# Scaling the probability rows on ScalarE instead of VectorE in a fused attention and gated adapter kernel

## The reference, cut to what matters

```python
q = (xn @ wq.T)   # 32 heads of 128;  k, v: 8 heads of 128, each shared by 4 query heads
q, k = rope(q), rope(k)
scores = q k^T / sqrt(128) * key_scale + causal
probs  = softmax(scores)
attn   = probs @ v
s = attn @ wo.T
x = x + s * silu(mixture_of_rank_16_adapters(xn))
```

## Time and profile before

| | us |
|---|---|
| median of 3 runs | 1474.9 (1472.89 to 1476.49) |
| span of the profiled execution, from its first instruction to its last | 1473.0 |
| TensorE busy | 1372.8 (93%) |
| VectorE busy | 1196.0 (81%) |
| ScalarE busy | 809.3 (55%) |
| GpSimd busy | 423.0 (29%) |

### The profile page before, as it was taken

How to read it: one execution, slowest core, us unless ns; L and a number is a source line. 1 busy time by engine, 2 the same in 40 slices (tenths; PEclk the granted TensorE clock), 3 DMA queues, 4 the chain that set the end, 5 groups by cost and what they waited for, 6 DMA issues and landing times.

```text
span 1473.0 us, 23326 instructions
## 1 busy us (share of the span) xinstructions
PE 1372.8 (93%) x6982; PEld 1130.1 (77%) x6982; DVE 1196.0 (81%) x3022; ACT 809.3 (55%) x2064; POOL 423.0 (29%) x340
## 2 busy tenths in 40 slices
PE   6699999999998999989999999999999999999997
PEld 5577667788777887778777887778877787877785
DVE  6976768878889887888888788887787888888887
ACT  4445555555555665556555555556555565555563
POOL 4311123221434123241342213331233312423231
PEclk9799999999999999999999999999999999999999
DMA  5000021000001000000000000000000000001223
GB/s 196 22 12 1 22 72 65 22 7 0 21 21 28 0 7 21 14 28 0 14 28 21 7 0 21 21 28 0 2 26 14 28 0 14 22 13 64 79 71 136
DMA packets 23291, 43.33 MB, mean 29 GB/s; under 512 B 2464, under 2 KB 2592, under 8 KB 23264
## 3 DMA queue, kind: packets, MB, share of 16 engines
q1 hardware_dynamic: 20736, 37.90, 8.0%
q10 hardware_dynamic: 2528, 5.11, 0.9%
HBM read 34.61 MB, written 8.39 MB: 29 GB/s over the span
## 4 chain that ended last, share of the span: by engine, by line
PE 49%; issue 21%; DVE 18%; POOL 8%; ACT 3%; DMA 0%; POOLq 0%; DVEq 0%; ACTq 0%
PE o_ps L542 13%; PE bank_b L450 12%; PE bank_a L450 7%; PE s_ps L517 5%; PE pv_ps L532 4%; POOL rot L366 3%; DVE probs L1126 3%; PE t_ps L625 3%; POOL w_lo L359 3%; DVE probs L1079 2%; POOL w_hi L356 2%; PE s_ps L512 2%; DVE cosx L999 2%; DVE cosx L989 2%; DVE q_lo L1005 2%
## 5 line engine op out<-in xcount | busy, mean ns | idle before, releaser
L366 POOL TENSOR_TENSOR rot<-rot,tab 128x512 f32<-128x512 f32 x160 | 209.6, 1310 | 921.3 <-ACT rot L730 921.3
L800 ACT ACTIVATE probs<-probs,row_min 128x128 f32<-128x128 f32 (+1 forms) x512 | 227.1, 445 | 122.1 <-DVE row_min L1079 120.9
L1126 DVE TENSOR_SCALAR probs<-probs,row_inv 128x128 f32<-128x128 f32 (+1 forms) x512 | 208.5, 470 | 4.5
L450 PE MATMUL bank_b<-xT_hi,w_hi 128*128 (+1 forms) x508 | 205.3, 404 | 0.5 <-POOL w_lo L373 0.5
L542 PE MATMUL o_ps<-w_hi,attn_hi 128*128 128x512 f32 x500 | 198.9, 398 | 7.2 <-POOL w_lo L359 4.0
L450 PE MATMUL bank_b<-xT_hi,w_lo 128*128 (+1 forms) x508 | 199.8, 393 | 0.0
L450 PE MATMUL bank_b<-xT_lo,w_hi 128*128 (+1 forms) x508 | 199.2, 392 | 0.0
L542 PE MATMUL o_ps<-w_lo,attn_hi 128*128 128x512 f32 x500 | 197.3, 395 | 0.0
L542 PE MATMUL o_ps<-w_hi,attn_lo 128*128 128x512 f32 x500 | 196.8, 394 | 0.0
L761 ACT ACTIVATE attn_hi<-pv_ps 128x512 fp32r<-128x512 f32 x128 | 76.4, 597 | 172.1 <-PE pv_ps L532 171.3
L625 PE MATMUL t_ps<-tab,probs 128*128 128x128 f32 x768 | 110.9, 282 | 49.1 <-DVE probs L1126 49.0
(11 more groups left out here) (151 smaller groups left out, 3094.8 us busy)
## 6 DMA issues: line engine op xcount, KB each, us to landing
raw<-w_seq SPq DMA_DIRECT2D x78, 256.0 KB, 2.6
gate_scratch<-silu ACTq DMA_DIRECT2D x16, 256.0 KB, 2.1
out<-y_sum SPq DMA_DIRECT2D x16, 256.0 KB, 2.0
raw<-x SPq DMA_DIRECT2D x13, 256.0 KB, 2.7
raw<-gate_scratch SPq DMA_DIRECT2D x13, 256.0 KB, 2.9
x_sb<-x SPq DMA_DIRECT2D x3, 1024.0 KB, 10.6
x_sb<-x SPq DMA_DIRECT2D x4, 256.0 KB, 5.7
tab<-tables ACTq DMA_DIRECT2D x1, 768.0 KB, 5.3
```

The costliest lines, as they stand in the source:

```text
L366: nc.gpsimd.tensor_tensor(v, v, tab[:, s:s + SEQ].unsqueeze(1).to_broadcast([P, 2, SEQ]), ALU.mult).then_inc(sin_done[kind], 1)
L450: mm = nc.tensor.matmul(dst, w(a, c), x[:, c, bass.ds(x0, BLOCK)], start=(c == 0 and n == 0), stop=(c == DC - 1 and n == 2))
L800: a = nc.scalar.activation(s, s, ACT.Exp, bias=row_min[:, i:i + 1], scale=-1.0, accum_out=row_sum[:, i:i + 1])
L1126: ins = nc.vector.tensor_scalar(s, s, row_inv[:, i:i + 1], None, ALU.mult)
```

## The change

The four multiplications of `probs` by `row_inv` leave `dve_unit` and come into `act_unit`, right behind the four exponents, as activations with a Copy and the reciprocal as their scale. ScalarE waits there for `inv_done`, which VectorE's reciprocal sets; the reciprocal itself stays on VectorE, and `probs_ready` is now set by ScalarE.

```diff
@@ act_unit
                 a.then_inc(exp_done, 1)
+                act.wait_ge(inv_done, n4[j + 1])
+                for h in range(2):
+                    for qt in range(2):
+                        s = probs[:, h, P * qt:P * qt + P * (qt + 1)]
+                        i = 2 * h + qt
+                        a = nc.scalar.activation(s, s, ACT.Copy, scale=row_inv[:, i:i + 1])
+                a.then_inc(probs_ready, 1)
@@ dve_unit
                 nc.vector.reciprocal(row_inv[:, :], row_sum[:, :]).then_inc(inv_done, 1)
-                dve.wait_ge(inv_done, n4[j + 1])
-                for h in range(2):
-                    for qt in range(2):
-                        s = probs[:, h, P * qt:P * qt + P * (qt + 1)]
-                        i = 2 * h + qt
-                        ins = nc.vector.tensor_scalar(s, s, row_inv[:, i:i + 1], None, ALU.mult)
-                ins.then_inc(probs_ready, 1)
```

## The result

The changed kernel takes 1577.34 us (median of 4 runs, 1574.22 to 1577.60) against 1474.91 us before (1472.89 to 1476.49). The ratio is 1.0695, with a 95% interval of 1.0679 to 1.071: slower by 7.0%. The forecast was 1493, slower by 1.2%, with a range up to 1518. The direction was right and the size wrong by a factor of more than five.

The account below looks back on a forecast made before the run. TensorE, busy 93%, was taken as the bound, so only its waits count. Terms 36 + 3 - 11 + 3 - 11 + 2 + 2 = +24, clock -9, leaning to +18 on 1473.0, median 1.9 above: 1493 us, range 1478 to 1518.

Parts of the forecast that it names:

- stretched, not late: VectorE's scalings at the three long transposes' waits per group (2.58, 1.90, 2.32 us) take 4.85 us instead of 1.01.
- The price of the scaling: On ScalarE, four scalings in a row take 1.06 us until the next instruction starts, priced from plain Copies.
- Part 1: Item j = 1, output bank: TensorE stalls 1.12 us, or 1.30 in a group's fourth unit, +36 us in all.
- Part 2: Item j = 3, queries: 3.96 us from reciprocal to first score; changes of +3, -11 and +3 us.
- Part 3: First unit of a group: 1.2 of the 2.58 us wait comes back, -11 us over eight.
- The clock: Of 24 us lost at TensorE's lower level, 9 us come back as stretches behind long waits go.
- Rival (b): New stalls of about 1.1 us in each of 31 units also drop the clock: +40, 1533 us; chance 0.05.
- The first group: Side work shares `o_ps` there: +2 us.
- Rival (a): Stretched scalings decide: their waits and lost clock go, no query stall follows, -34, 1441 us; chance 0.21 in both sizes.
- half size: Only half the gain from removing the stretched scalings is had: 1458 us; chance 0.21 shared with the full size.
- The dear end of the scaling: Four scalings on ScalarE priced like the exponents, end to end: 1.76 us, adding 39 us.
- sign of being wrong: Forecast wrong if the scaling takes 1.5 us or more, L542 rarely waits for L1041, or calm units' clock falls below 0.97.

Follow-up runs that it names:

- e2: Changed kernel with the scaling of item j = 1 alone back on VectorE: 1530.16 us, ratio 1.0407 to the kernel before.
- e3: Changed kernel with the scaling of item j = 3 alone back on VectorE: 1523.84 us, ratio 1.033 to the kernel before.
- e8: Changed kernel with the scalings of items 1 and 3 back on VectorE, 0 and 2 on ScalarE: 1457.22 us, ratio 0.9878 to the kernel before.
- e10: Kernel before with the scaling of item j = 2 alone on ScalarE, behind the exponents: 1456.16 us, ratio 0.9877.
- e1: Changed kernel with ScalarE's four scalings multiplying by the constant 0.5, not the reciprocal from a tile: 1537.78 us, ratio 1.0409 to the kernel before.
- e9: Changed kernel with GpSimd's sine product of H2 in item 3 waiting until H1's low part is done: 1578.56 us, ratio 1.0699 to the kernel before.
- e5: Changed kernel with VectorE's addition that frees the output bank put ahead of K's chain in item 1: 1569.23 us, ratio 1.0637 to the kernel before.
- e11: Kernel before with item 2's scaling on ScalarE behind the exponents, item 3's behind H2's swap and H1's high part: 1424.43 us, ratio 0.9657.
- e6: Changed kernel with ScalarE scaling behind the swap of K in item 1 and of H2 in item 3: 1451.27 us, ratio 0.9841 to the kernel before.
- e7: Kernel before with item 2's scaling on ScalarE behind the exponents and item 3's behind the swap of H2: 1440.41 us, ratio 0.9784.

## Why the prediction was wrong, point by point

**The reading of the places was right.** Both stalls stand where they were put: L542 behind L1048 in nearly every unit and the scores behind H1's low part in each item 3. e2, e3, e8 and e10 show that they are the whole of the loss. One reading was not right: the three long waits were called "stretched, not late". That holds for the first unit (4.85 us) and the third (3.95); in the fourth the scaling took 1.95 us, 0.94 over the 1.01 of the earlier trace rows, and the rest of the 2.32 came from the late reciprocal. The prediction let that wait move from the transposes to the scores. Measured are both, 2.09 and 2.33 us, and the transposes wait 22.3 us in all, not under 15.

**The price of the scaling was too low.** "I take 1.06, as the Copy is the same function": it was 1.50, and e1 shows why. The 0.407 us of the earlier trace rows is a Copy without a factor from a tile; such a factor adds 92 ns, four times. The right row stood in the same group: the exponents, whose bias is read from a tile, take 0.495 us for 256 columns, and the scaling takes 0.494. The Trainium skill has the rule ("ScalarE: Activation LUTs", section "What ACT_TABLE_LOAD costs"): 186 ns plus 0.833 per column, some 93 more for each pointer operand, and an overlap of some 93 between neighbours. By it the four take an estimated 2 x 0.386 + 2 x 0.492 - 3 x 0.093 = 1.48 us, and the trace agrees with its 1.50. The prediction used another page, whose 1.39 was nearer than its own 1.06.

**Part 1 was mis-sized by little.** Forecast 36 us, and L542's wait rose by 39.6 (1.39 us in a calm unit against 1.12, 2.19 against 1.30 + 0.47 in the fourth). But the item as a whole is worth 47 us in e2, 15 of them in the start and the first group, and none of them by the clock.

**Part 2 is the step that failed.** It gave 3.96 us from the reciprocal to the first score and so -5 us in all. Measured are 4.95 to 4.97 in each of the four kinds of unit: 0.44 is the scaling, and 0.50 the collision of H1's low part with the sine product, shown by e9. The prediction took 0.68 from the earlier trace rows for the low part without asking what would lie beside it once the swap had moved right ahead of it. The 3.67 of before has that collision in it, in the scaling's 2.12 us; the 3.96 was put together without any. With 4.95 the terms become 9 x 1.28 - 7 x 0.55 + 7 x 1.46 = +18, 23 us more, and the eight first units get 0.99 each as well, +8.

**Part 3 held its gain, but not beside part 2.** e10 shows 18 us for item 2 alone, against the forecast 11 and a share of the clock. In the change the wait of 2.58 is gone, but item 3 of the same unit stalls 2.33.

**The clock went the other way.** Forecast -9 us, measured +20 by the grant and +22 by the busy time: a miss of some 30, as large as that of part 2. Rival (b), that new stalls drop the clock, had a chance of 0.05. Stalls of 2.0 to 2.3 us in every unit take the place of three per group, and e8 gives back 34.6 us of matmul time without them. But which stall costs how much stays open: in the later groups the grant is 0.97 with and without the change, and e5 and e2 lose clock although stalls were taken away. e5 and e11 show how far it can go, 1411.0 and 1348.7 us for the same matmuls.

**The first group** lost 17.7 us with the start, and the forecast had 2 for its side work over the other terms. e2 gives 15.3 of them back, so it is item 1's chain that meets the side work. TensorE waits there for `o_ps` up to 2.7 us at L498. Part 2 with 31 us, the clock with some 30 and part 1 with 4 make 65 of the 85 us that the forecast missed; this stretch has a part of the rest, which wasn't taken apart further.

**The chances.** Rival (a), faster, had 0.21. Its half size, 1458, exists, but only in kernels that keep the two chains free: e8 and e10 have 1457 and 1456, and e6, e7 and e11 are faster still. The dear end of the scaling, 1.76, lay above the truth, yet the range was cut at 1518. Even at that end the sum would have been 1473.0 + 15 + 39 + 1.9 = 1529, since the collision was in no term and the clock's term had the wrong sign. The prediction's own sign of being wrong, a scaling of 1.5 us or more, came true.

## What to carry to other kernels

Work that moves to another engine's queue is paid for by what stands behind it there, not by that engine's share of busy time: the same 512 scalings cost +7.0% ahead of two swaps and brought -1.6% behind them. When a chain moves in time, look at what will run beside each of its links on the engine that it shares a resource with, and take the price of an instruction from a row with the same operands (here a factor read from a tile), not from one with the same name. New stalls in a loop can cost clock beyond their own sum, here 22 us on 81, and taking away one of two need not bring it back; leave room for that in the range.

## What the runs showed of the hardware

- A per-row factor read from a tile costs ScalarE 92 ns per instruction over a constant one (494 against 402 ns for 256 columns, 395 against 303 for 128).
- VectorE's subtraction of 512 columns takes 1.19 us in place of 0.68 when it starts beside a GpSimd product (875.78 against 875.14 to 876.41). Before, VectorE's four scalings took 2.12 us beside the same product, and 4.85 beside splits, against 1.01. ScalarE's took 1.50 beside a split too (858.61 to 860.11, the split from 858.79 to 860.09), and none of its 512 took more than 0.498.
- The grant can be lower with fewer stalls: e5 has 42.5 us less of one wait and a clock of 0.944 against 0.961, and e2 39.8 us less and 0.951. Why isn't shown.
